# Slot block of a four-stage network: value bias as a matmul, value weights' low parts formed in the second attention, kv affine on two engines, logits ahead of the next hidden layer

## Chip, cores and metric

One core of one Trainium2 chip. The metric is the device time of one execution in microseconds, the median of three runs. Engines are named as in the profile: PE (TensorE), ACT (ScalarE), DVE (VectorE), POOL (GpSimd), SP (SyncE, which here only issues DMAs).

## The reference

Four residual steps on `x` of shape (8, 256, 256) with a context of the same shape:

```python
x = x + tanh(g_xattn[0]) * attention_16_heads(layernorm(x), ctx)
x = x + tanh(g_ffn[0])   * slot_block(layernorm(x))
x = x + tanh(g_xattn[1]) * attention_8_heads(keys and values from ctx and x, queries from x)
x = x + tanh(g_ffn[1])   * int8_like_gated_ffn(layernorm(x))
```

The change touches the second step and the start of the third. The second step, with 64 slots of width 256:

```python
h = gelu(ctx @ w1.T + b1)
route_logits = (h @ w2.T + b2) / (abs(tau) + 0.1)
topk_w = softmax(top 8 of the 64 logits);  alpha = topk_w on those slots, 0 elsewhere
slot_input = einsum('bts,btd->bsd', alpha, x)
gi = slot_input / (alpha.sum(axis=1) + 1e-8)
r, z, n = GRU gates of gi and the slots S
S_new = (1 - z) * n + z * S
slot_values = S_new @ wv.T + bv
out = einsum('bts,bsd->btd', alpha, slot_values) @ wo.T + bo
```

In the third step the keys and values come from `Wkv` (256 x 2048, keys in its first half, values in its second), applied to the context and to the latents, both normed and scaled by `gamma` and `beta` per column; queries come from `Wq`.

## The kernel before

`program` runs four blocks, one behind the other, with a barrier of all engines between them: `attention0`, `slots0`, `attention1`, `ffn1`. Within a block each engine has its own list of instructions, written out by hand, and semaphores between the lists. An engine runs its list strictly in order, so an instruction that waits holds up all behind it.

`slots0` (L951 to L1516) works on four pairs of batches, `p` = 0 to 3, each 512 tokens. The steps and who does them:

- `turn_x(p)` (PE, L1352) transposes the normed tokens, `x_out(p)` (ACT) copies them out, `hidden(p)` (PE, L1360) multiplies by `w1`, `gelu(p)` (ACT, L1056), `logits(p)` (PE, L1368) multiplies by `w2`.
- `logits_out`, `top_eight` (DVE) add `b2` and find the eight largest; `exps(p)` (ACT, L1061); `weights(p)` (DVE, L1190 to L1198) makes `alpha`; `gather(p)` (PE, L1379) forms the slot inputs. gelu and exp use different activation tables, so ACT loads a table between them.
- `gates_of(p)` (PE, L1401 to L1406), `gate_input` (DVE, L1247), `sigmoid` (ACT, L1080), `candidate` (DVE), `tanh` (ACT), `new_slots(p)` (DVE).
- `turn_slots(p)` (PE, L1413), `slots_out(p)` (ACT, L1088), `project_out(p)` (PE, L1419) with `wv` and `wo` folded into one matrix, `slot_values(p)` (DVE, L1268) which adds the folded bias `bvo` and moves the values out of PSUM, `mixture(2p)` and `mixture(2p+1)` (PE, L1427), `residual(b)` (DVE, L1273).
- Meanwhile the block prepares the next one. SP loads `Wq` and `Wkv` into `raw1`; `high(i)` (ACT, L1070, L1072) rounds each of six chunks of 1024 elements per partition to the float32r format, and `low(i)` (DVE, L1280) forms what the rounding left over. Chunks 4 and 5 are the value weights. `c_norm` and `c_apply` (DVE) norm batch 0, `turn_kv(c)` (PE, L1456) transposes it, `kv_affine(c)` (ACT, L1101, L1105) scales it into `kvf` and rounds it, `kv_low(c)` (DVE, L1239) forms its low part.

The order on DVE from the fourth gate input on is, in the code:

```python
            gate_input(3)
            candidate(2)
            new_slots(1)
            low(4)
            candidate(3)
            slot_values(0)
            new_slots(2)
            low(5)
            residual(0)
```

`attention1` begins on PE with keys and queries of two heads (`project_k` L2063, `project_q` L2078), the scores of head 0, and then the first `project_v` (L2089), which reads the value weights. DVE begins with `k_low(0, 0)` (L1813). SP loads a context batch, `bo` and `Wo`, and then the feed-forward weights into the tensors `wih` and `whh`, which `slots0` does not use.

## Time and profile before

| | us |
|---|---|
| median of three runs (lowest, highest) | 895.93 (894.72, 896.11) |
| the profiled execution, its own time | 898.05 |
| span of its trace | 895.9 |
| PE busy in the span | 823.7 (92%) |
| DVE busy | 669.3 (75%) |
| ACT busy | 590.2 (66%) |
| `attention0` | 0 to 213 |
| `slots0` | 213 to 281.5 |
| `attention1` | 281.5 to about 790 |
| `ffn1` | the rest |

A row of the timeline gives the start in us from the span's start, how long the instruction or the merged group lasted, the engine, the line of the kernel, the operation, output and inputs with their shapes, and in brackets how long the engine had been idle and who ended the wait. Successive instructions of an engine overlap a little: the next one starts 0.05 to 0.2 us before the one before it is recorded as done. The granted clock (PEclk) is given as a share of PE's full 2.4 GHz; 0.50 is its lower level, 1.2 GHz.

### The profile page before, as it was taken

To read this page: it belongs to the slowest core of one execution; us is meant where nothing else is said; L and a number is where in the kernel's file an instruction comes from. 1 tells how busy PE (TensorE), PEld (TensorE's weight loads), DVE (VectorE), ACT (ScalarE), POOL (GpSimd) and SP (SyncE) were. 2 spreads that over 40 slices of the span, in tenths; PEclk is the share of its full clock that TensorE was granted. 3 is DMA by queue.
4 is the path that set the end of the run, shared out by engine and by line. 5 is a ranking of instruction groups with operands and counts; after the bars stand their busy time and mean duration, and the time that the engine had idled before them with its cause. 6 is when DMAs were issued, how large, how long until landed. Compare 5 with 4: busy or idle time off the path is not lost. (4 is left out here: it accounts for less than half of the span.)

```text
span 895.9 us, 17186 instructions
## 1 busy us (share of the span) xinstructions
PE 823.7 (92%) x5671; PEld 665.7 (74%) x5671; DVE 669.3 (75%) x1527; ACT 590.2 (66%) x1205; POOL 91.9 (10%) x169
## 2 busy tenths in 40 slices
PE   5899999997886899999999999999899999997757
PEld 5677777665555687888888788888788888885323
DVE  5677888786795778887877686877686877775487
ACT  4366666663733686777787677777577777775663
POOL 4111111010000000100000000000000000000556
PEclk9699999998988999999999999999999999999698
DMA  5832322423103200000000000000000000000002
GB/s 136 143 117 96 98 95 72 139 79 146 9 0 114 61 1 1 13 1 1 13 1 1 16 2 1 13 1 1 16 2 1 1 1 1 1 1 0 1 1 94
DMA packets 37914, 33.41 MB, mean 37 GB/s; under 512 B 10240, under 2 KB 36544, under 8 KB 37568
## 3 DMA queue, kind: packets, MB, share of 16 engines
q1 hardware_dynamic: 37568, 31.76, 12.1%
q0 software_dynamic: 256, 0.52, 0.4%
q8 instruction: 47, 0.77, 0.4%
q14 instruction: 43, 0.35, 0.1%
HBM read 17.59 MB, written 2.10 MB: 22 GB/s over the span
## 5 line engine op out<-in xcount | busy, mean ns | idle before, releaser
L1845 DVE TENSOR_REDUCE c_neg_max<-c_pS 128x1 f32<-128x512 f32 x128 | 88.3, 690 | 70.3 <-PE c_pS L2102 68.9
L1676 ACT ACTIVATE c_probs<-c_pS,c_neg_max 128x512 f32<-128x512 f32 x128 | 88.2, 689 | 62.1 <-DVE c_neg_max L1845 62.1
L547 DVE TENSOR_REDUCE a_neg_max<-a_pS 128x2 f32<-128x512 f32 x128 | 82.4, 686 | 17.1 <-PE a_pS L770 16.6
L1694 ACT ACTIVATE c_probs<-c_probs,c_r_sum 128x512 f32<-128x512 f32 x128 | 92.5, 722 | 3.7 <-DVE c_r_sum L1851 2.9
L400 ACT ACTIVATE a_probsT<-a_pT 128x512 f32<-128x512 f32 x128 | 69.6, 597 | 33.6 <-PE a_pT L786 32.5
L2063 PE MATMUL c_pK<-c_kv,w_hi 128*128 128x512 f32 x256 | 82.9, 406 | 4.6 <-PEq L1515 4.0
L1829 DVE TENSOR_TENSOR c_pT_lo<-c_pT,c_pT_hi 128x512 fp32r<-128x512 f32 x128 | 86.9, 680 | 0.0
L2089 PE MATMUL c_pK<-w_hi,c_kv 128*128 128x512 f32 x248 | 78.9, 399 | 3.2 <-DVE c_k_lo L1813 3.2
L2119 PE MATMUL c_pO<-c_pT_hi,c_v_hi 128*128 128x256 f32 x256 | 77.3, 302 | 3.1 <-DVE c_pT_lo L1829 3.1
L2109 PE MATMUL c_pT<-ident,c_probs 128*128 128x128 f32 x512 | 76.8, 272 | 0.0
L2109 PEld LDWEIGHTS c_pT<-ident,c_probs 128*128 128x128 f32 x512 | 63.6, 140 | 17.5 <-ACT c_probs L1694 0.6
L1684 ACT CAST c_pT_hi<-c_pT 128x512 fp32r<-128x512 f32 x128 | 73.6, 576 | 0.0
L2119 PE MATMUL c_pO<-c_pT_hi,c_v_lo 128*128 128x256 f32 x256 | 72.3, 282 | 0.0
L2119 PE MATMUL c_pO<-c_pT_lo,c_v_hi 128*128 128x256 f32 x256 | 72.1, 282 | 0.0
L2063 PEld LDWEIGHTS c_pK<-c_kv,w_hi 128*128 128x128 f32 x256 | 49.4, 194 | 17.2 <-issue 4.4
L1824 DVE TENSOR_TENSOR c_v_lo<-c_pK,c_v_hi 128x512 fp32r<-128x512 f32 x62 | 42.9, 692 | 21.5 <-ACT c_v_hi L1669 21.5
L1813 DVE SCALAR_TENSOR_TENSOR c_k_lo<-c_pK,c_bk,c_k_hi 128x512 fp32r<-128x512 f32 x64 | 47.3, 739 | 15.3 <-ACT c_k_hi L1658 15.2
L2089 PEld LDWEIGHTS c_pK<-w_hi,c_kv 128*128 128x128 f32 x248 | 45.3, 188 | 18.0 <-DVE c_k_lo L1813 8.3
L1689 ACT ACTIVATE c_oT_hi<-c_pO,c_bv 128x256 fp32r<-128x256 f32 x64 | 30.4, 476 | 41.1 <-PE c_pO L2119 36.6
L2102 PE MATMUL c_pS<-c_k_hi,c_q_hi 128*128 128x512 f32 x128 | 52.8, 412 | 5.0 <-issue 5.0
L2078 PE MATMUL c_pQ<-c_kv,w_hi 128*128 128x256 f32 x256 | 53.8, 303 | 0.0
L2063 PE MATMUL c_pK<-c_kv,w_lo 128*128 128x512 f32 x128 | 51.5, 402 | 0.0
(395 smaller groups left out, 2081.4 us busy)
## 6 DMA issues: line engine op xcount, KB each, us to landing
a_q_stack<-w_hi SPq DMA_DIRECT2D x94, 64.0 KB, 2.6
a_k_stack<-w_hi SPq DMA_DIRECT2D x48, 64.0 KB, 2.6
c_kv<-w_hi SPq DMA_DIRECT2D x42, 64.0 KB, 2.6
s_ctx<-in_ctx_dram SPq DMA_DIRECT2D x8, 256.0 KB, 2.8
x_sb<-in_x_dram SPq DMA_DIRECT2D x8, 256.0 KB, 3.0
b_raw<-in_L_xattn_Wkv_dram SPq DMA_DIRECT2D x1, 2048.0 KB, 12.6
ctx_in<-in_ctx_dram SPq DMA_DIRECT2D x8, 256.0 KB, 2.6
out_dram<-x_sb SPq DMA_DIRECT2D x8, 256.0 KB, 2.2
```

The costliest lines, as they stand in the source:

```text
L400: nc.scalar.activation(probsT[:, r // 2 % 2, 2 * (r % 2) + e, :, :], pT[:, e, :, :], ACT.Exp).then_inc(s["exp"], 1)
L547: nc.vector.tensor_reduce(neg_max[:, r // 2 % 2, :, e, r % 2], pS[:, e, :, :], AX_X, ALU.max, negate=True).then_inc(s["max"], 1)
L1676: nc.scalar.activation(probs[:, u % 2, :], pS[:, u % 2, :], ACT.Exp, bias=neg_max[:, u % 4:u % 4 + 1], accum_out=sums[:, u % 4:u % 4 + 1]) ...
L1684: nc.scalar.copy(pT_hi[:, :, half], pT[:, u % 2, :].rearrange("p (t q) -> p t q", q=P)).then_inc(s["T_hi"], 1)
L1694: nc.scalar.mul(probs[:, u % 2, :], probs[:, u % 2, :], r_sum[:, u % 4:u % 4 + 1]).then_inc(s["probs"], 1)
L1829: nc.vector.tensor_tensor(pT_lo[:, :, half], pT[:, u % 2, :].rearrange("p (t q) -> p t q", q=P), pT_hi[:, :, half].bitcast(F32), ALU.subtr ...
L1845: nc.vector.tensor_reduce(neg_max[:, u % 4:u % 4 + 1], pS[:, u % 2, :], AX_X, ALU.max, negate=True).then_inc(s["max"], 1)
L2063: last = nc.tensor.matmul(pK[:, :], W[x][:, c, INNER + h * DH:INNER + (h + 1) * DH], kv[par][:, y, c, :], start=(c == 0 and i == 0), stop= ...
L2078: last = nc.tensor.matmul(pQ[:, 0:T], W[x][:, c, h * DH:(h + 1) * DH], kv[par][:, y, c, T:KEYS], start=(c == 0 and i == 0), stop=(c == DC ...
L2089: last = nc.tensor.matmul(bank[:, :], kv[par][:, y, c, kt * P:(kt + 1) * P], W[x][:, c, 2 * INNER + half * 512:2 * INNER + (half + 1) * 51 ...
L2109: last = nc.tensor.transpose(pT[:, u % 2, t * P:(t + 1) * P], probs[:, u % 2, t * P:(t + 1) * P], ident[:, :])
L2119: last = nc.tensor.matmul(pO[:, 0:T], (v_hi, v_lo)[x][:, h // 4, t, (h % 4) * DH:(h % 4 + 1) * DH], (pT_hi, pT_lo)[y][:, t, :], start=(t = ...
```

## The change

Five edits:

1. PE issues `logits(p)` ahead of `hidden(p+1)`; the instructions are the same.
2. The folded value bias is put in PSUM by a matmul with the identity, ahead of the projection; ACT (`val_out`) copies the values out, and DVE's `slot_values` is gone.
3. The value half of `Wkv` goes to two further tensors (`raw_v`, the storage of `wih` and `whh`) by two DMAs, `high(4)` and `high(5)` become two casts each, and `low(4)` and `low(5)` leave the block. `attention1` forms these low parts at the head of DVE's list; its first `project_v` of each half waits for them, and so does SP before it loads the feed-forward weights over `raw_v`.
4. `kv_affine` of column 1 is done by DVE; ACT keeps column 0 and both roundings.
5. ACT does `sigmoid(3)` ahead of `tanh(2)`.


```diff
             sp.dma_start(raw1[:, :, 0:INNER], a["L1_xattn_Wq"].rearrange("(c p) n -> p c n", p=P)).then_inc(s["raw"], DMA)
-            sp.dma_start(raw1[:, :, INNER:3 * INNER], a["L1_xattn_Wkv"].rearrange("(c p) n -> p c n", p=P)).then_inc(s["raw"], DMA)
+            sp.dma_start(raw1[:, :, INNER:2 * INNER], a["L1_xattn_Wkv"][:, 0:INNER].rearrange("(c p) n -> p c n", p=P)).then_inc(s["raw"], DMA)
+            for c in range(DC):
+                sp.dma_start(raw_v[c], a["L1_xattn_Wkv"][c * P:(c + 1) * P, INNER:2 * INNER]).then_inc(s["raw_v"], DMA)
...
-                if hi <= INNER:
+                if lo >= 2 * INNER:
+                    if i == 4:
+                        act.wait_ge(s["raw_v"], 2 * DMA)
+                    for c in range(DC):
+                        last = nc.scalar.copy(w1_hi[:, c, lo:hi], raw_v[c][:, lo - 2 * INNER:hi - 2 * INNER])
+                    last.then_inc(s["raw_hi"], 1)
+                elif hi <= INNER:
...
+            def val_out(p):
+                act.wait_ge(s["val"], p + 1)
+                nc.scalar.copy(val[:, p, :], ps[:, p, 0:D]).then_inc(s["val_sb"], 1)
...
             sigmoid(2)
+            sigmoid(3)
             tanh(2)
+            val_out(0)
             slots_out(1)
-            sigmoid(3)
             tanh(3)
+            val_out(1)
             slots_out(2)
+            val_out(2)
             slots_out(3)
-            kv_affine(0)
-            kv_affine(1)
+            kv_affine()
+            kv_high(0)
+            val_out(3)
+            kv_high(1)
...
+            def kv_affine():
+
+                dve.wait_ge(s["kv"], 2)
+                dve.wait_ge(s["snew"], 2)
+                for side in range(2):
+                    last = nc.vector.tensor_scalar(kvf[:, 1, side * T:(side + 1) * T], ps[:, 4, side * T:(side + 1) * T], cols["gamma"][:, side, 1:2],
+                                                   cols["beta"][:, side, 1:2], ALU.mult, ALU.add)
+                last.then_inc(s["kvf1"], 1)
...
             new_slots(1)
-            low(4)
             candidate(3)
-            slot_values(0)
             new_slots(2)
-            low(5)
             residual(0)
...
             def project_out(p):
                 pe.wait_ge(s["snewT_sb"], p + 1)
+                nc.tensor.matmul(ps[:, p, 0:D], ident[:, :], bvo[:, :], start=True, stop=False)
                 for k in range(DC):
-                    last = nc.tensor.matmul(ps[:, p, 0:D], snewT[:, p, k * P:(k + 1) * P], wvo[:, k * D:(k + 1) * D], start=(k == 0), stop=(k == DC - 1))
+                    last = nc.tensor.matmul(ps[:, p, 0:D], snewT[:, p, k * P:(k + 1) * P], wvo[:, k * D:(k + 1) * D], start=False, stop=(k == DC - 1))
...
             turn_x(2)
+            logits(0)
             hidden(1)
-            logits(0)
             turn_x(3)
+            logits(1)
             hidden(2)
-            logits(1)
+            logits(2)
             hidden(3)
-            logits(2)
             logits(3)
...
+            sp.wait_ge(s["w_lo"], 2)
             full = (FT - 1) * P
...
+            for half in range(2):
+                lo, hi = 2 * INNER + half * 512, 2 * INNER + (half + 1) * 512
+                for c in range(DC):
+                    last = nc.vector.tensor_tensor(w_lo[:, c, lo:hi], raw_v[c][:, half * 512:(half + 1) * 512], w_hi[:, c, lo:hi].bitcast(F32), ALU.subtract)
+                last.then_inc(s["w_lo"], 1)
...
                 half, kt = divmod(j, KT)
+                if isinstance(n, int) and n == 0 and kt == 0:
+                    pe.wait_ge(s["w_lo"], half + 1)
```

PE's list in the router, before: transposes of the tokens (from `ident,xn`), the hidden layer (from `b_xT,s_w1T`) and the logits (from `s_w2T,b_hT`).

```order
L1352 MATMUL b_ps<-ident,xn 128x128 x8
L1360 MATMUL b_ps<-b_xT,s_w1T 128x512 x2
L1368 MATMUL b_ps<-s_w2T,b_hT 128x64 x4
L1352 MATMUL b_ps<-ident,xn 128x128 x8
L1360 MATMUL b_ps<-b_xT,s_w1T 128x512 x2
L1368 MATMUL b_ps<-s_w2T,b_hT 128x64 x4
L1360 MATMUL b_ps<-b_xT,s_w1T 128x512 x2
L1368 MATMUL b_ps<-s_w2T,b_hT 128x64 x8
L1434 MATMUL b_ps<-s_whhT,s_ctx 128x512 x2
```

And after:

```order
L1370 MATMUL b_ps<-ident,xn 128x128 x8
L1386 MATMUL b_ps<-s_w2T,b_hT 128x64 x4
L1378 MATMUL b_ps<-b_xT,s_w1T 128x512 x2
L1370 MATMUL b_ps<-ident,xn 128x128 x8
L1386 MATMUL b_ps<-s_w2T,b_hT 128x64 x4
L1378 MATMUL b_ps<-b_xT,s_w1T 128x512 x2
L1386 MATMUL b_ps<-s_w2T,b_hT 128x64 x4
L1378 MATMUL b_ps<-b_xT,s_w1T 128x512 x2
L1386 MATMUL b_ps<-s_w2T,b_hT 128x64 x4
L1453 MATMUL b_ps<-s_whhT,s_ctx 128x512 x2
```

The third group of logits now stands between the last two hidden layers, and each group of logits stands directly behind the transposes or the hidden layer whose output ACT has to turn into its input.

DVE's list in the tail, before, from the last sums of the gate inputs' new slots on: `w1_lo` is a low part of the weights, `b_lm<-b_ps,s_bvo` a value with its bias, `b_ex` new slots.

```order
L1264 TENSOR_TENSOR b_ex<-b_ex_top,b_hT 128x256
L1280 SCALAR_TENSOR_TENSOR w1_lo<-b_raw1,w1_hi 128x2x512
L1252 TENSOR_TENSOR b_hT<-b_xT,s_gh_n 128x256
L1255 TENSOR_TENSOR b_hT<-b_ps,b_hT 128x256
L1268 TENSOR_TENSOR b_lm<-b_ps,s_bvo 128x256
L1260 TENSOR_TENSOR b_ex_top<-s_hs,b_hT 128x256
L1262 TENSOR_TENSOR b_ex_top<-b_ex_top,b_xT 128x256
L1264 TENSOR_TENSOR b_ex<-b_ex_top,b_hT 128x256
L1280 SCALAR_TENSOR_TENSOR w1_lo<-b_raw1,w1_hi 128x2x512
L1273 SCALAR_TENSOR_TENSOR x_sb<-b_ps,gates,x_sb 128x512
```

And after:

```order
L1291 TENSOR_TENSOR b_ex<-b_ex_top,b_hT 128x256
L1279 TENSOR_TENSOR b_hT<-b_xT,s_gh_n 128x256
L1282 TENSOR_TENSOR b_hT<-b_ps,b_hT 128x256
L1287 TENSOR_TENSOR b_ex_top<-s_hs,b_hT 128x256
L1289 TENSOR_TENSOR b_ex_top<-b_ex_top,b_xT 128x256
L1291 TENSOR_TENSOR b_ex<-b_ex_top,b_hT 128x256
L1296 SCALAR_TENSOR_TENSOR x_sb<-b_ps,gates,x_sb 128x512
```

The two low parts and the addition of the bias are gone; the candidate of pair 3, the new slots of pair 2 and the first residual follow one another.

DVE's list at the seam of the two blocks, after: the affine of column 1 (`b_xT` is `kvf`), the low parts of batch 0 (`c_kv0`), and behind the two branches the head of `attention1`.

```order
L1354 TENSOR_SCALAR c_bq<-c_bq 128x8
L1260 TENSOR_SCALAR b_xT<-b_ps,c_gamma,c_beta 128x256 x2
L1266 TENSOR_TENSOR c_kv0<-b_xT,c_kv0 128x512
L1296 SCALAR_TENSOR_TENSOR x_sb<-b_ps,gates,x_sb 128x512 x2
L1266 TENSOR_TENSOR c_kv0<-b_xT,c_kv0 128x512
L957 UNCONDITIONAL_BRANCH
L1784 UNCONDITIONAL_BRANCH
L2015 TENSOR_TENSOR w1_lo<-wih,w1_hi 128x512
L2015 TENSOR_TENSOR w1_lo<-whh,w1_hi 128x512
L2015 TENSOR_TENSOR w1_lo<-wih,w1_hi 128x512
L2015 TENSOR_TENSOR w1_lo<-whh,w1_hi 128x512
L1833 SCALAR_TENSOR_TENSOR c_k_lo<-c_pK,c_bk,c_k_hi 128x512
```

Before, nothing stood between the branches and the first `c_k_lo`, and no `b_xT` was written here.

## Rows read from the trace of the kernel before

**Rows 1.** The page, its first line.

```profile
span 895.9 us, 17186 instructions
```

**Rows 2.** The slot block in the table by stretches (columns: stretch, length, busy time by engine).

```profile
213.00:281.50 68.50, 54.76 (x252) 35.52 (x252) 52.16 (x170) 34.18 (x62) 3.30 (x8) 0.88 0.17 51
```

**Rows 3.** Timeline, PE in the router (start us, us, what, idle before).

```profile
223.30 1.88 PE L1360 MATMUL b_ps<-b_xT,s_w1T 128*128 128x512 f32 x4
225.02 1.00 PE L1368 MATMUL b_ps<-s_w2T,b_hT 128*128 128x64 f32 x8
225.86 1.94 PE L1360 MATMUL b_ps<-b_xT,s_w1T 128*128 128x512 f32 x4
...
233.19 1.10 PE L1379 MATMUL b_ps<-xn,b_alpha 128*64 128x257 f32 x8 [1.74 <-DVE b_alpha L1198]
```

**Rows 4.** Timeline, ACT in the router.

```profile
227.83 0.69 ACT L1056 ACTIVATE b_hT<-b_ps,s_bias 128x512 f32<-128x512 f32 x1 [1.92 <-PE b_ps L1360]
228.54 1.28 ACT L1061 ACT_TABLE_LOAD   x1
229.84 3.18 ACT L1061 ACTIVATE b_ex<-b_lm,b_neg_top,s_tau 128x128 f32<-128x128 f32 x8
```

**Rows 5.** Timeline, DVE in the router.

```profile
231.51 0.43 DVE L1190 TENSOR_TENSOR b_ex_top<-b_ex 128x256 f32<-128x256 f32 x1 [0.74 <-ACT b_ex L1061]
```

**Rows 6.** Stretches of 3 us; PEclk is the third column from the end.

```profile
234.00:237.00 3.00, 2.61 (x15) 1.02 (x11) 2.83 (x20) 3.00 (x6) 0.00 (x0) 0.66 0.02 5
240.00:243.00 3.00, 3.00 (x14) 2.14 (x14) 2.83 (x10) 2.81 (x4) 0.00 (x0) 1.00 0.00 0
258.00:261.00 3.00, 2.34 (x11) 1.53 (x9) 2.90 (x7) 0.42 (x1) 0.00 (x0) 1.00 0.00 0
264.00:267.00 3.00, 3.00 (x12) 1.94 (x9) 2.95 (x5) 0.00 (x0) 0.00 (x0) 0.50 0.00 0
```

**Rows 7.** Groups by line, DVE, 241.5 to 281.5 us.

```profile
L1280 DVE SCALAR_TENSOR_TENSOR w_lo<-b_raw,w_hi 128x1024 fp32r<-128x1024 f32 x6 | 7.3, 1216 | 0.0
...
L1268 DVE TENSOR_TENSOR b_lm<-b_ps,s_bvo 128x256 f32<-128x256 f32 x4 | 1.7, 413 | 0.0
...
L1208 DVE TENSOR_SCALAR b_hT<-b_ps,b_r_wsum 128x256 f32<-128x256 f32 x2 | 1.0, 484 | 0.1
```

**Rows 8.** Timeline, DVE in the tail of the slot block.

```profile
257.79 0.69 DVE L1247 TENSOR_TENSOR b_xT<-b_ps,s_gh_rz 128x512 f32<-128x512 f32 x1 [0.53 <-PE b_ps L1401]
...
261.98 0.42 DVE L1252 TENSOR_TENSOR b_hT<-b_xT,s_gh_n 128x256 f32<-128x256 f32 x1 [0.33 <-ACT b_xT L1080]
...
274.53 1.41 DVE L1273 SCALAR_TENSOR_TENSOR x_sb<-b_ps,gates,x_sb 128x512 f32<-128x512 f32 x2 [0.58 <-PE b_ps L1427]
...
277.74 0.69 DVE L1239 TENSOR_TENSOR c_kv<-b_xT,c_kv 128x512 fp32r<-128x512 f32 x1 [1.40 <-ACT c_kv L1105]
...
279.67 0.68 DVE L1239 TENSOR_TENSOR c_kv<-b_xT,c_kv 128x512 fp32r<-128x512 f32 x1
```

**Rows 9.** Timeline, PE in the tail of the slot block.

```profile
248.37 0.59 PE L1404 MATMUL b_ps<-s_bih,ident 128*128 128x256 f32 x2
248.81 1.03 PE L1406 MATMUL b_ps<-s_wihT,b_turned 128*128 128x256 f32 x4
...
263.25 2.09 PE L1427 MATMUL b_ps<-b_lm,b_turned 64*128 64x256 f32 x8 [2.24 <-DVE b_lm L1268]
...
273.36 1.14 PE L1427 MATMUL b_ps<-b_lm,b_turned 64*128 64x256 f32 x8 [2.49 <-DVE b_lm L1268]
```

**Rows 10.** Timeline, start of the second attention: PE and DVE.

```profile
281.54 1.19 PE L2063 MATMUL c_pK<-c_kv,w_hi 128*128 128x512 f32 x2 [4.03 <-PEq L1515]
...
289.26 0.73 PE L2089 MATMUL c_pK<-w_hi,c_kv 128*128 128x512 f32 x2 [0.16 <-DVE c_k_lo L1813]
...
285.20 0.75 DVE L1813 SCALAR_TENSOR_TENSOR c_k_lo<-c_pK,c_bk,c_k_hi 128x512 fp32r<-128x512 f32 x1 [4.85 <-ACT c_k_hi L1658]
```

More of the change, by code:

```diff
@@ L1092, in values_out, with kv_high @@
                 nc.scalar.copy(wvo, ps[:, 3, :]).then_inc(s["wvo_sb"], 1)
[L1094 to L1099 removed]
+            def val_out(p):
+                act.wait_ge(s["val"], p + 1)
+                nc.scalar.copy(val[:, p, :], ps[:, p, 0:D]).then_inc(s["val_sb"], 1)
+            def kv_affine():
+                act.wait_ge(s["kv"], 1)
+                act.wait_ge(s["cols"], 7 * DMA)
+                act.wait_ge(s["snew"], 2)
                 for side in range(2):
[L1101 to L1102 removed]
+                    last = nc.scalar.activation(kvf[:, 0, side * T:(side + 1) * T], ps[:, 0, side * T:(side + 1) * T], ACT.Identity,
+                                                bias=cols["beta"][:, side, 0:1], scale=cols["gamma"][:, side, 0:1])
                 last.then_inc(s["kvf"], 1)
[L1104 removed]
+            def kv_high(c):
+                act.wait_ge(s[("kvf", "kvf1")[c]], 1)
                 nc.scalar.copy(c_kv[:, 0, c, :], kvf[:, c, :]).then_inc(s["kv_hi"], 1)
@@ L1330, in _ @@
             residual(3)
-            slot_values(2)
             c_apply(2, of_lat, 1, "latn")
@@ L1580, in attention1 @@
         pQ = pb("c_pQ", [P, 512])
-        names = """load next wo wo_hi wo_lo const ctx stats moments var rstd ctxn lat stats_l var_l rstd_l latn kv kvf kv_hi
+        names = """w_lo load next wo wo_hi wo_lo const ctx stats moments var rstd ctxn lat stats_l var_l rstd_l latn kv kvf kv_hi
                    kv_lo k k_hi k_lo q q_hi q_lo v v_hi v_lo S max exp rsum probs T T_hi T_lo O oT_hi oT_lo X ob res stats_o
@@ L2537, in program @@
                 attention0(nc, a, x_sb, ident, gates, {k: v[:] for k, v in gru.items()}, slot, xn, (w1_hi, w1_lo, c_kv))
-                slots0(nc, a, x_sb, ident, gates[:, 2:3], {**slot, "wv": gru["wv"][:]}, xn, w1_hi, w1_lo, ctx_in, clips, c_kv, c_cols)
+                slots0(nc, a, x_sb, ident, gates[:, 2:3], {**slot, "wv": gru["wv"][:]}, xn, w1_hi, w1_lo, ctx_in, clips, c_kv, c_cols, raw_v)
             ident_b = split_w.enter_context(nc.sbuf_tensor("ident_b", [P, P], BF16))
```

26 lines of the change are left out of this document (8 added, 18 removed).

## The prediction

> **What bounds the kernel now.** I read the page first, then the table by stretches, and then the timelines of TensorE (PE), ScalarE (ACT) and VectorE (DVE) over the slot block, asking at each gap who ended it. The profiled execution spans 895.9 us [rows 1], and the change lies almost wholly in the slot block, 213.0 to 281.5 us, where PE is busy 54.8 of 68.5 us and DVE 52.2 [rows 2]: here no engine is full, and what counts is a chain that runs from one to the next. The second attention behind it is left alone but for its first microseconds, so whatever the slot block gains or loses should pass into the time one for one.
>
> The block has two parts for this purpose. In the **router** (to about 233 us) the last link is ACT: it computes the gelu of the four pairs, and only after the fourth can it load the table for exp (1.28 us) and begin the exponentials [rows 4]. DVE waits 0.74 us for the first of them [rows 5], and PE then sits idle for 1.74 us until the first weights `alpha` are there [rows 3]. So gelu(3) starts everything that follows, and gelu(3) waits for hidden(3), which PE begins at 225.86 [rows 3]. In the **tail** (from gate_input(3) at 257.79 [rows 8]) DVE is nearly always busy, and the block ends with DVE's kv_low(1), from 279.67 for 0.68 us. Its only waits there are 0.33, 0.58 and 1.40 us [rows 8]; PE waits 2.24 and 2.49 us for slot values that DVE adds the bias to [rows 9].
>
> **Part 1, logits ahead of the next hidden layer.** Until now PE does hidden(p+1) while ACT does gelu(p), so that logits(p) finds its input ready. Now logits(p) stands first. For p = 0 and 1 another turn_x lies between and little is waited for. For p = 2 nothing does. By PE's rows: turn_x(3) still ends at about 223.4; logits(1) takes 0.85 us (from 225.02 to the next start at 225.86 [rows 3]) and now runs to 224.25; hidden(2) has 1.88 us [rows 3], to 226.15; gelu(2) takes 0.69 us like its sister [rows 4], to 226.9, with PE idle for some 0.9 us; logits(2) 0.85 us, to 227.75; and hidden(3) begins there instead of at 225.86. That is **1.9 us later**, and gelu(3), the table load, the exponentials and `alpha` come as much later. What DVE gains, since logits(0) and logits(1) reach it 1.6 us sooner, is lost, because its next step, weights(0), waits for the exponentials. I see no slack that takes up the 1.9 us: from 231.5 on the four engines pass the work on to each other, and PE's idle 1.74 us is the wait for this very chain. So gather(0), the gates and gate_input(3) move from 257.79 to about 259.7.
>
> **Part 2, low parts of the value weights moved away.** low(4) and low(5) leave DVE's tail: two of the six instructions of 1216 ns [rows 7], 1.14 us each counted to the next start (rows of one engine overlap by some 0.08 us), **2.3 us**. They become four subtractions of 128x512 at the head of the second attention. The nearest row is kv_low, 0.69 us for the same form [rows 8], so 2.5 to 2.8 us in all. There DVE is idle for 4.85 us, of which 3.7 us after the first instruction of PE at 281.54, until the first k_low at 285.20 [rows 10]. I take them at nothing; were this cover gone they would cost up to 2.8 us. The first projection that reads these low parts starts at 289.26 [rows 10], 4 us after they are ready. The new wait stands in SP's queue before the feed-forward weights; they and the load of w_down behind them go out 1 to 2 us later, behind the first three loads of the block, and DVE asks for them only at unit 9 of 16 of the first batch. On ACT high(4) and high(5) become two casts of 128x512 each; both lie between waits of over 2 us. SP issues two DMAs more in the slot block, each 0.4 to 0.6 us of its queue, ahead of loads that are used 20 us later or more: nothing.
>
> **Part 3, bias by a matmul.** The four additions of slot_values leave DVE: 413 ns each [rows 7], 0.34 us counted to the next start, **1.3 us**. PE gets four matmuls with the identity; the same thing for `bih` takes 0.59 us and 0.44 us to the next start [rows 9]. ACT gets four copies of 128x256 out of PSUM. What matters more is that PE no longer has to stand in line behind 1.2 us of low() and the candidate on DVE: its 2.24 and 2.49 us of idle time [rows 9] shrink to the ACT copy of some 0.4 us, though 0.44 us of bias matmul goes in again each time.
>
> **Part 4, affine on two engines, sigmoid(3) ahead.** DVE takes column 1: two tensor_scalar of 128x256 from PSUM, at most 0.48 us each by the form [rows 7], **0.8 us** added. It ends the 1.40 us in which DVE waited for ACT [rows 8], since ACT starts column 0 while DVE is still at the residuals. sigmoid(3) earlier removes the wait of 0.33 us, and the 0.58 us goes with PE's earlier mixtures. That is **2.3 us of waits**; I leave 0.5 us of them in place for the last hand-over, PE's turn_kv to DVE.
>
> **The sum.** Tail: -2.3 (low) -1.3 (bias) -2.3 (waits) +0.8 (affine) +0.5 = -4.6 us. Router: +1.9 us. Together **-2.7 us**. The profiled execution took 898.05 us against a median of 895.93 us of the runs shown, 2.1 us more; so the profiled execution of the new kernel would be about 895.4 and its median **893.2 us**. A measurement of this kernel tells a difference of about 0.2%, 1.8 us, from none.
>
> **What the clock may do to it.** PE's granted clock was 0.66 (a mixture of the levels 2.4 and 1.2 GHz) in 234 to 237, behind the idle 1.74 us, and 0.50, that is 1.2 GHz, in 264 to 267, behind the idle 2.24 us [rows 6]. At 1.2 GHz eight matmuls of a pair of mixtures take 2.09 us, at 2.4 GHz 1.14 us [rows 9]. In the sum I have taken the second spell as gone, because the idle time before it goes, and the first as it was. This is the choice that moves the number most.
>
> **The rivals.** *The slow spell in the tail stays* (0.17). From the first mixture to the end of turn_kv PE has three pairs of mixtures, three projections with bias, two turns and eight transposes: 3.2 + 3.9 + 0.6 + 1.0 = 8.7 us, with the four short waits for ACT about 10.2, against 10.6 us of DVE. A spell of 4 us as before adds about 2 us; turn_kv comes 1.4 us late, and DVE waits at its affine. Then -1.3 us, 894.6.
>
> *The new wait cools PE in the router* (0.10). PE idles some 0.9 us before logits(2) and again before logits(3). If hidden(3) and logits(3) run at 1.2 GHz, 1.72 and 0.85 us become twice that: 2.6 us more on the chain, -0.1 us in all, 895.8. Against it: in 258 to 261 PE was idle for 0.66 of 3 us, and the clock stayed at 1.00 [rows 6]. [...]
>
> *Slower: the clock is low over the router and the gates too* (0.07). Besides those 2.6 us, gates_of(0) would take twice its time: two matmuls of 128x512, 1.72 us as in hidden() (223.30 to 225.02 [rows 3]), 0.44 us for the bias and 0.86 us for two of half the width, 3.0 us, and DVE's gate_input(0) waits for it. -2.7 + 2.6 + 3.0 = +2.9, 898.8. It decides from 4.5 us of extra time on PE's chain on. Against: up to now the clock was back at 1.00 in 240 to 243 [rows 6], before the gates.
>
> *The low parts are not covered in the second attention* (0.03): up to 2.8 us given back, +0.1 at worst, 896.0. For it: DVE would have to start late behind the barrier.
>
> *The reorder is free* (0.08): if hidden(3) were not held up, or gelu(3) not the start of the chain, the tail's gain stands alone, -4.6, 891.3. The rows speak against it.
>
> **How the numbers follow.** The forecast has 0.55, with about 0.8 us to either side for the unknown rests (0 to 1 us of hand-over, 0.7 to 1.0 us of affine). Faster by over 0.2% takes most of it, the free reorder and a little of the slow spell: 0.60. Within: its upper edge, most of the slow spell, the cooled router, the uncovered low parts: 0.32. Slower: 0.08. The range 891.2 to 895.5 reaches from the free reorder to short of the cooled router and leaves out 0.2.
>
> **What would show it.** Right: PE idle of about 0.9 us before logits(2), hidden(3) and gelu(3) 1.9 us later, gather(0) at about 235.1, gate_input(3) at about 259.7; DVE without a gap from there to the affine; the block's last DVE instruction ending at about 277.6; four subtractions on DVE done before 285; granted clock 1.0 from 261 to 270. Wrong: gelu(3) within 0.5 us of 227.83; a wait of over 1 us on DVE for turn_kv; PE below 0.9 of its clock in 243 to 257; the first k_low later than 4 us after the block's start.

## The result, and the profile after

The changed kernel takes **901.84 us** (median of 6 runs, 901.22 to 902.17), the kernel before beside it 896.34 us (6 runs, 894.72 to 897.83): ratio 1.0061, 95% interval 1.0044 to 1.0078. So it is 5.5 us slower, where the forecast was 2.7 us faster. The profiled execution took 901.61 us. Its page, the span and the two queues that carry instructions (packets, MB, share), answers to [rows 1]; the two queue lines of before are 47 packets, 0.77 MB and 43, 0.35.

```profile
span 899.6 us, 17209 instructions
...
q8 instruction: 47, 0.77, 0.4%
...
q14 instruction: 44, 0.35, 0.1%
```

The slot block first. The router, timelines of PE and ACT in after, beside [rows 3, 4]:

```profile
227.56 1.10 PE L1386 MATMUL b_ps<-s_w2T,b_hT 128*128 128x64 f32 x8 [0.78 <-ACT b_hT L1058]
228.50 1.94 PE L1378 MATMUL b_ps<-b_xT,s_w1T 128*128 128x512 f32 x4
231.22 1.10 PE L1386 MATMUL b_ps<-s_w2T,b_hT 128*128 128x64 f32 x8 [0.78 <-ACT b_hT L1058]
...
230.48 0.69 ACT L1058 ACTIVATE b_hT<-b_ps,s_bias 128x512 f32<-128x512 f32 x1 [2.97 <-PE b_ps L1378]
231.18 1.28 ACT L1063 ACT_TABLE_LOAD   x1
232.48 3.18 ACT L1063 ACTIVATE b_ex<-b_lm,b_neg_top,s_tau 128x128 f32<-128x128 f32 x8
```

PE waits 0.78 us before logits(2) and hidden(3) starts at 228.50. gelu(3) starts at 230.48 against 227.83 [rows 4]; the block began 0.42 us later, so the reorder costs 2.2 us here. Then the granted clock, stretches of 3 us as in [rows 6]:

```profile
237.00:240.00 3.00, 2.61 (x12) 1.06 (x11) 2.86 (x20) 3.00 (x7) 0.00 (x0) 0.66 0.03 5
240.00:243.00 3.00, 2.17 (x11) 1.07 (x10) 2.54 (x9) 2.98 (x7) 0.00 (x0) 0.50 0.00 0
243.00:246.00 3.00, 3.00 (x14) 2.23 (x11) 1.81 (x7) 2.54 (x5) 0.00 (x0) 0.70 0.00 0
...
264.00:267.00 3.00, 2.77 (x16) 1.76 (x16) 2.86 (x8) 1.09 (x3) 0.00 (x0) 1.00 0.00 0
```

Behind the wait for `alpha` PE now stays low for about 9 us, where before it was back at 1.00 in 240 to 243; in the tail it never falls. And the tail, DVE, then the PE and ACT rows that one of its waits goes back to, beside [rows 8, 9]:

```profile
261.86 0.69 DVE L1274 TENSOR_TENSOR b_xT<-b_ps,s_gh_rz 128x512 f32<-128x512 f32 x1 [0.53 <-PE b_ps L1419]
...
275.65 0.99 DVE L1260 TENSOR_SCALAR b_xT<-b_ps,c_gamma,c_beta 128x256 f32<-128x256 f32 x2
276.81 0.69 DVE L1266 TENSOR_TENSOR c_kv<-b_xT,c_kv 128x512 fp32r<-128x512 f32 x1 [0.17 <-ACT c_kv L1118]
278.27 1.41 DVE L1296 SCALAR_TENSOR_TENSOR x_sb<-b_ps,gates,x_sb 128x512 f32<-128x512 f32 x2 [0.77 <-PE b_ps L1446]
279.60 0.68 DVE L1266 TENSOR_TENSOR c_kv<-b_xT,c_kv 128x512 fp32r<-128x512 f32 x1
...
277.11 1.14 PE L1446 MATMUL b_ps<-b_lm,b_turned 64*128 64x256 f32 x8 [1.60 <-ACT b_lm L1104]
...
276.17 0.62 ACT L1118 CAST c_kv<-b_xT 128x512 fp32r<-128x512 f32 x1
276.69 0.37 ACT L1104 COPY b_lm<-b_ps 128x256 f32<-128x256 f32 x1
```

From gate_input(3) to DVE's last end it is 261.86 to 280.28, 18.42 us, against 257.79 to 280.35, 22.56: the tail is 4.14 us shorter. What is left in it is a wait of 1.60 us on PE for val_out(3), which ACT has in its queue behind the affine and the first high part; DVE waits 0.77 us for that mixture in turn. The four subtractions at the head of the second attention are free: they run from 281.48 to 284.07, and the first value projection starts at 289.16 against 289.26 [rows 10].

So the block gives back what it wins: +2.2 (router) +1.4 (clock, gather(0) to gate_input(3)) -4.1 (tail) = -0.5 us, and with its start 0.42 us later the second attention begins at 281.48 against 281.54 [rows 10]. **The 5.5 us arise elsewhere**, 215 us further on. A loop of the second attention (batches 1 to 6, two to a turn) jumps back twice. PE's rows at the two jumps, before and then after:

```profile
497.36 0.47 PE L2102 MATMUL c_pS<-c_k_hi,c_q_hi 128*128 128x512 f32 x1 [2.18 <-issue]
631.50 0.76 PE L2102 MATMUL c_pS<-c_k_hi,c_q_hi 128*128 128x512 f32 x1 [2.86 <-issue]
```

```profile
497.38 0.76 PE L2129 MATMUL c_pS<-c_k_hi,c_q_hi 128*128 128x512 f32 x1 [2.31 <-issue]
500.05 0.80 PE L2129 MATMUL c_pS<-c_k_lo,c_q_hi 128*128 128x512 f32 x1 [1.91 <-issue]
...
634.08 0.77 PE L2129 MATMUL c_pS<-c_k_hi,c_q_hi 128*128 128x512 f32 x1 [2.61 <-issue]
636.75 0.79 PE L2129 MATMUL c_pS<-c_k_lo,c_q_hi 128*128 128x512 f32 x1 [1.90 <-issue]
```

"issue" means that PE waited for nothing the trace shows. One such wait per jump has become two, and the view of waits (us in total, times, longest) sums them up, before and after:

```profile
PE c_pS L2102 <- issue: 5.0, 2, 2.9
```

```profile
PE c_pS L2129 <- issue: 8.7, 4, 2.6
```

Aligned instruction by instruction, ACT in after is 0.1 us ahead from 286 to 490, 2.8 us behind from 503 to 620, and 5.6 us behind from 637 on: the two jumps cost 5.7 us more than before. (Behind the last attention 1.8 us of it come back, with the granted clock of 821 to 841 at 0.86 instead of 0.61, so that these two profiled spans differ by 3.7 us and the medians by 5.5.) None of the code there was changed. What did change is the length of PE's list ahead of that loop. From the compiled lists (index of the loop's first instruction; the loop is 1795 instructions long on PE, 347 on DVE):

```
                                    PE     DVE
before                              4558   775
after                               4576   776
```

Four fp32 matmuls with the identity are 4 instructions each, and two waits are added (those of the first `project_v` of each half): 18. The packets of the page don't tell the two kernels apart, 47 and 47: both load instructions at each jump, and only the waits by "issue" show that after waits twice for them.

### The profile page after: what moved, and what is told of

It reads as the page before. It is cut to its first block and busy times, and to the rows that moved or that the text cites. A ratio compares the mean times of both kernels' runs of the same rounds, so it can differ in the third digit from the quotient of the medians.

```text
span 899.6 us, 17209 instructions
## 1 busy us (share of the span) xinstructions
PE 824.3 (92%) x5677; PEld 665.7 (74%) x5679; DVE 669.7 (74%) x1527; ACT 590.4 (66%) x1209; POOL 92.5 (10%) x169
## 5 line engine op out<-in xcount | busy, mean ns | idle before, releaser
L2088 PEld LDWEIGHTS c_pK<-c_kv,w_hi 128*128 128x128 f32 x256 | 49.5, 194 | 16.4 <-issue 3.6
L2129 PE MATMUL c_pS<-c_k_lo,c_q_hi 128*128 128x512 f32 x128 | 51.3, 401 | 3.8 <-issue 3.8
```

What stands on the lines that cost most here:

```text
L2088: last = nc.tensor.matmul(pK[:, :], W[x][:, c, INNER + h * DH:INNER + (h + 1) * DH], kv[par][:, y, c, :], start=(c == 0 and i == 0), stop= ...
L2129: last = nc.tensor.matmul(pS[:, u % 2, :], (q_hi, q_lo)[x][:, slot, qs], (k_hi, k_lo)[y][:, slot, :], start=(i == 0), stop=(i == 2))
```

## The experiments

**Theory F**: each engine fetches its instructions in blocks, and at a jump back it stalls, or not, by where the loop stands in its list; the change only moved it. The rivals were that the new work itself (another wait, a load going out later, the clock) carries into the loop, and for the slot block those of the prediction. In all kernels below the added matmuls write one PSUM column that nobody reads; nothing of the computation is left out in any of them.

### Move PE's list alone

The kernel before, with four matmuls of one column at the end of the slot block's PE list (head of the loop at 4574):

```diff
             mixture(7)
+            pe.wait_ge(s["res"], 4)
+            for _ in range(4):
+                nc.tensor.matmul(ps[:, 5, 0:1], ident[:, :], ident[:, 0:1], start=True, stop=True)
```

> The kernel before, with four one-column matmuls (16 PE instructions in the compiled list) added at the very end of the slot block, where PE idles for over 3 us. Nothing else is changed. Theory F (fetch): what made the changed kernel slower in the second attention is that its 18 extra PE instructions moved the head of PE's loop to just ahead of a border of the instruction stream's fetched pieces, so PE stalls twice on each jump back; then this kernel, moved by 16, shows the second stall of 1.6 to 1.9 us behind the first or second matmul of the iteration on both jumps, and is 3.3 to 4 us slower than before, near 900. Rival W (work): the loss comes from what the change does (waits for low parts, later feed-forward loads, clock); then this kernel takes the time of before, 896.3, within 0.5 us, with one stall per jump.

Measured: **902.66 us** (5 runs, 900.97 to 903.13), ratio 1.0071 [1.0058, 1.0084]. PE at the first jump:

```profile
496.73 0.72 PE L2105 MATMUL c_pS<-c_k_hi,c_q_hi 128*128 128x512 f32 x1 [2.18 <-issue]
...
499.95 0.80 PE L2105 MATMUL c_pS<-c_k_hi,c_q_lo 128*128 128x512 f32 x1 [2.06 <-issue]
```

Sixteen instructions that do nothing make before as slow as after, with a second stall at both jumps (2.06 and 1.49 us). By the medians it is 6.5 us where 3.3 to 4 were expected; aligned with before, this execution loses 5.4 us at the two jumps, after 5.7. Theory F holds, and the change's own work is not needed for the loss. The second stall stands before the third matmul behind the jump here (head at 4574) and before the second in after (head at 4576), which is the same place of the list: index 4583, the weight load of that matmul.

After, with three such matmuls (head at 4588):

> The changed kernel, with three one-column matmuls (12 PE instructions) added at the end of the slot block. Theory F: the loop's head moves past the border, the second stall is gone on both jumps, and the time falls by 3.5 to 4 us from the changed kernel's, to about 898. Rival W: within 0.5 us of the changed kernel, 901.8.

Measured: **892.71 us** (9 runs, 890.49 to 896.03), ratio 0.9960 [0.9947, 0.9973]: 9.1 us less than after, by adding work. I had expected one stall per jump to go; both went, and PE has no issue wait in the loop at all. The page of the profile shows where they went:

```profile
q8 instruction: 29, 0.48, 0.2%
```

29 packets instead of 47. 0.77 MB over 47 packets is 16.4 KB each; 7626 instructions of 64 bytes are 29.8 such blocks, so 29 is the list fetched once, and 18 more are nine blocks for each jump. The Trainium skill (Runtime: NRT & Kernel Launch, section "Instruction fetch mechanics") has the blocks of 256 instructions and says that a taken branch whose target isn't in the current two-block window must fetch it first. The packet size agrees; the two-block window does not: here a loop of seven blocks came back twice without one packet. The same section gives PE's instruction memory as 2048 instructions, which is eight blocks, and that figure fits.

Further places, for the kernel before with 7 and with 24 matmuls (4586, 4654), and the fastest version at that time with 12 (4624):

> The kernel before with seven one-column matmuls (28 PE instructions) and a wait added at the end of the slot block's PE list, so that the head of PE's loop in the second attention stands 28 instructions later, 2 short of where it stands in the stall-free run (after with 3 such matmuls). Theory F (the two jumps back of PE's loop cost by where the head stands, whatever the kernel does): no issue stall of PE at 497 and 632 us, and 2.2 + 2.9 = 5.1 us less than before, about 891 us; since those lie beside half-filled stretches, 3 to 6 us less count. Then the change itself, compared at equal place with the 892.7 us of after with 3 matmuls, is worth between -2 and +2 us. Rival S (the stalls went in that run through the change's own reordering, and not through the place): before keeps one stall per jump, 896 us, or gets two, 902 us.

Measured: **894.11 us** (12 runs, 891.86 to 897.73), ratio 0.9983 [0.9969, 0.9996]. 29 packets, no stall on PE, but only 1.8 us won, not 5: DVE now shows a wait of its own at both jumps,

```profile
497.75 0.69 DVE L1848 TENSOR_REDUCE c_neg_max<-c_pS 128x1 f32<-128x512 f32 x1 [3.58 <-issue]
...
629.73 0.69 DVE L1848 TENSOR_REDUCE c_neg_max<-c_pS 128x1 f32<-128x512 f32 x1 [3.66 <-issue]
```

which in before was covered by the one of PE.

> The kernel before with 24 one-column matmuls (96 PE instructions): the head of the loop 96 instructions later than in before. They take about 24 x 0.06 = 1.5 us on PE at the slot block's end. Theory F with a border (stalls are worst with the head just ahead of a border of 256 instructions, none from just behind it): still no issue stall at the jumps, since the next border is 184 instructions further, and 891 + 0.5 to 1.5 us. Rival (what counts is not a border but the very alignment of the head): one or two stalls per jump, 897 to 904 us.

Measured: **900.07 us** (10 runs, 897.28 to 902.91), ratio 1.0053 [1.0039, 1.0068]. One stall per jump (2.40 and 2.29 us), 48 packets: the "still none" of theory F with a border is wrong. And the matmuls are dearer than I had reckoned:

```profile
278.24 6.14 PE L1515 MATMUL b_ps<-ident 128*128 128x1 f32 x48
```

0.26 us for a matmul (two records each) against the 0.06 us assumed (the four matmuls of the first run had taken 1.05 us already); the second attention starts 4.0 us late, and that is the whole difference from before.

> The fastest version so far with 12 instead of 3 one-column matmuls: 36 PE instructions more ahead of the loop, about 1.1 us more on PE while the vector engine still works, so nearly free. Its head stands between that of the stall-free runs (0 stalls) and that of before plus 24 (one stall per jump). Theory F narrow (stall-free only where the loop's end lies just behind a border, since further in the next block is fetched as well): one stall per jump, 47 or 48 packets on the first instruction queue, 891 to 893 us. Theory F wide (stall-free over a good part of a block): 29 packets, 886.5 to 887.5 us.

Measured: **892.00 us** (6 runs, 891.62 to 892.96), against 886.53 with three: 47 packets, one stall per jump. The stall-free place is narrow: seen at 4586 and 4588, not at 4576 nor at 4624.

The times at which the packets of the first instruction queue start, in the traces, show more. At the first jump they start at 494.46 and 497.72 in before, whose one stall ends at 497.36, and at 494.37 and 497.75 in after, whose stalls end at 497.38 and 500.05. So after waits for the second packet too: with its head seven instructions ahead of 4583 it reaches that border at once. After with three matmuls has no packet between 477 and 759. If a block of 256 begins at 4583, another begins at 6375, and the loop (head + 1795) ends 4 to 22 instructions ahead of that border in the kernels with the head at 4558 to 4576, 6 and 8 behind it at the stall-free 4586 and 4588, 44 and 74 behind it at 4624 and 4654. In the latter two a packet starts 4.4 and 5.3 us before those of the first jump (486.11, 493.20). All this fits an engine that holds eight blocks and loads one ahead: at 4558 to 4576 the head's block is the ninth and gone, and the jump loads nine; just behind the border it is the eighth and still there, unless the next load ahead goes out before the jump. The border and the eight blocks are worked out from these runs after the fact, and no run was made to test them.

### The router's order alone

Before with the new order of logits and hidden, nothing else:

```diff
-            hidden(1)
             logits(0)
+            hidden(1)
...
-            hidden(3)
             logits(2)
+            hidden(3)
```

> The kernel before with the order of the logits of the changed kernel and nothing else; the number of PE instructions is that of before. The chain through gelu(3) says: gelu(3) 2.2 to 2.7 us later, the gates 2.2 us later if PE's clock behaves as before and up to 4 us if the slow spell is as long as in the changed kernel; 898.5 to 900.3. If the reorder were free, 896.3.

Measured: **901.41 us** (6 runs, 897.04 to 902.50), ratio 1.0048 [1.0029, 1.0067]. From the block's start to gelu(3) 16.29 us, as in after (16.27) and against 14.04 in before. From gather(0) to gate_input(3) 26.04 us, against 24.60. The latter is the longer slow-clock spell: over all profiled kernels that distance takes only two values, 24.6 (13 kernels) and 26.0 to 26.2 (5); all three kernels with the new order have the long one, of fifteen with the old order two have it. So the reorder costs 2.2 us, and in these executions 1.4 us more by the clock; that it brings the longer spell about is likely by these counts, but not shown, since the old order can have it as well. The median lies above the expected 898.5 to 900.3: 5.3 us over before, of which these two make 3.6. The profiled execution (902.48 us) began the block 1.7 us later than that of before; the rest of the median's excess is open.

After with the old order put back:

> The changed kernel with the old order of logits and hidden layers. Its tail should be 4 us shorter than before's and its router as before's; the slot block ends 3.5 to 4.5 us earlier than before's, but the loop's head stands where it does in the changed kernel, so by theory F it gives back 3.8 us in the second attention: 896 to 897. By rival W (loss from the waits for low parts) likewise about 896 to 897; by a rival in which the reorder causes the stalls, 892.

Measured: **898.77 us** (6 runs, 897.25 to 900.24), ratio 1.0030 [1.0018, 1.0042]: 3.1 us less than after, but above the 896 to 897 that was expected. The second attention starts at 278.53, 3.0 us before before's (not 3.5 to 4.5: the last mixtures ran at a granted clock of 0.50 here, 2.08 us instead of 1.14), and the kernel is still slower than before, with two stalls at each jump. That is the whole case in one run.

Both together, old order and three matmuls:

> After with the old order of the logits and three one-column matmuls: the tail's gain without the router's loss, at the stall-free place. Measured so far: old order makes after 3.0 us shorter (898.8 against 901.8 us), the place makes it 9.1 us shorter (892.7 against 901.8 us). Theory F (router order and loop place add up): 892.7 - 3.0 = 889.7 us, range 888.5 to 891, second attention starting at 278.5 us, no issue stall at the jumps. Rival (the gain of the slot block is used up on the way, as a wait for something that doesn't start earlier): second attention 3 us earlier but the end within 1 us of 892.7 us.

Measured: **887.76 us** (6 runs, 886.57 to 889.53), ratio 0.9913 [0.9893, 0.9933]. The tail's gain arrives: the second attention starts 3.7 us earlier than in before, and PE has no stall. It is 0.7 us less than the range expected.

### The parts of the tail

Lengths here are from gate_input(3) to the end of DVE's last instruction of the block (before 22.56 us), since they don't depend on the clock in the router.

> Before with one part of the change, the value weights' low parts formed in the second attention (two subtractions of 1.22 us leave the slot block's vector list), and seven one-column matmuls, which put the loop's head where it stands in the stall-free runs. Compared with before plus seven (894.1 us, last vector instruction of the slot block ending at 280.3). By the prediction's term for low (-2.3) and the slow spell in the tail that then goes or stays (-1 to -2 more): last vector end 276.5 to 278, time 890.5 to 892. Rival (the wait for PE takes it over, since residual(0) is then waiting for mixture(0)): end at 279.5 or later, time within 0.8 us of 894.1. By theory F no issue stall at the two jumps and 29 packets on the first instruction queue.

Low parts alone: tail 21.51 us, **-1.05** where the sum had -2.3; 892.18 us (12 runs, 890.08 to 897.72), ratio 0.9957 [0.9941, 0.9973]. PE's wait for DVE's bias addition has its full length and the clock falls behind it as before:

```profile
265.97 1.14 PE L1433 MATMUL b_ps<-b_lm,b_turned 64*128 64x256 f32 x8 [2.24 <-DVE b_lm L1276]
266.00:269.00 3.00, 3.00 (x14) 2.07 (x14) 2.83 (x9) 0.03 (x1) 0.00 (x0) 0.73 0.00 0
```

(The second row is the stretch's clock, 0.73.) Where the other half of the gain went stands in DVE's row for candidate(3):

```profile
264.70 0.43 DVE L1260 TENSOR_TENSOR b_hT<-b_xT,s_gh_n 128x256 f32<-128x256 f32 x1 [1.47 <-ACT b_xT L1088]
```

Its wait for ACT's sigmoid(3) was 0.33 us in before [rows 8]; it has grown by 1.14 us, exactly one low(). So the first of the two low parts stood beside a wait, and its time is won only together with edit 5 of the change, sigmoid(3) ahead, which this run leaves out. In after DVE has no wait there. The end of the last vector instruction, 282.01, is that of the rival (279.5 or later), but this execution also lost 1.1 us in the router and 1.5 us by the long slow-clock spell; the time lies 0.2 us above the other forecast.

> Before with the bias part alone (identity matmul on PE, copy on ACT, four additions of 0.42 us off the vector engine) and three one-column matmuls for the loop's head. By the prediction's term (-1.3): last vector end about 279.0 against 280.3, time 892.8. Rival (bias off the vector engine gains nothing while the low parts still stand there and PE's tail gets four matmuls more): end 279.8 to 280.8, time within 0.5 us of 894.1; rival (val_out(3) ahead of the affine on ACT delays the kv chain): end after 280.8. No issue stall at the jumps, 29 packets.

Bias alone: tail 20.27 us, **-2.29**. DVE's rows add it up: the four additions 1.4, the wait of 0.58 us for the mixtures gone, and the wait for ACT's kv_high 1.08 instead of 1.40 us. So the term of -1.3 was right, and 0.9 us of the waits belong to this part. (This run has val_out(3) ahead of the affine, which after has not; what that order is worth follows below.) PE's waits of 2.24 and 2.49 us are gone (the longest left is 1.58), and the clock stays at 1.00 through the tail. Its time is 887.01 us (6 runs), ratio 0.9899 [0.9884, 0.9914], 7 us under the comparable kernel with low and bias as before, and that is more than the slot block gives. Its DVE list is four instructions shorter (771), DVE's issue wait at the jumps is gone, and the second instruction queue has ten packets fewer. This profiled execution has one stall of PE left:

```profile
q8 instruction: 38, 0.62, 0.3%
q14 instruction: 33, 0.27, 0.1%
```

```profile
627.86 0.47 PE L2106 MATMUL c_pS<-c_k_hi,c_q_hi 128*128 128x512 f32 x1 [3.80 <-issue]
```

38 is 29 and nine, and the times of the same kernel fall in two groups, 886.57 to 887.07 (four) and 891.57 and 892.93 (the profiled one). At this place of the list (4586) the fetch is sometimes needed and sometimes not: this one execution has both, nothing at the first jump and a fetch at the second. There two packets start within 0.4 us (623.08 and 623.50), where the jumps of before and after have one; by the reading above the first is the load ahead, gone out just before the jump. That is argued, not tested.

Next, the old order and three matmuls, with ACT's val_out(3) ahead of its affine, which takes away PE's 1.60 us:

```diff
             slots_out(3)
+            val_out(3)
             kv_affine()
             kv_high(0)
-            val_out(3)
             kv_high(1)
```

> As the run with the old logits and three matmuls, and ACT's val_out(3) ahead of its affine and high part of the contexts' keys. In after PE's mixture(6) waited 1.60 us for it. Theory V (that wait is in the path to the end of the slot block): residual(6) and (7) come 1 to 1.6 us earlier, the kv chain 0.6 us later (one copy ahead of it on ACT), the block ends 0.5 to 1.3 us earlier, 888.4 to 889.2 us if the other run gives 889.7. Rival (the kv chain ends the block as well): block's end unchanged or 0.5 us later, time within 0.5 us of the other run.

Measured: **886.53 us** (5 runs, 886.10 to 887.82), ratio 0.9902 [0.9882, 0.9922]; tail 17.56 us against 18.43 without the move. Theory V holds with 0.9 us by the tails; the times of the two kernels overlap.

The same with both halves of the affine on ACT again, as before the change:

> The fastest version so far (old logits order, three matmuls, val_out(3) early: 886.5 us) with the affine of both channels halves back on ACT, so without the change's split. By the prediction's term the split costs 0.8 us on the vector engine (0.99 us busy) and takes one link of 1.1 us out of ACT's chain: without it the last vector end is 0.5 us later to 0.8 us earlier, 885.7 to 887.0 us. Rival (vector engine would wait 1 us for kv_high(1) before its last subtraction): 887 to 888 us.

Measured: **885.36 us** (4 runs, 883.69 to 885.56), ratio 0.9875 [0.9859, 0.9892]; tail 17.57 us. The split of the affine is worth nothing: DVE saves 0.99 us of work and waits 1.07 us for ACT instead. The 1.2 us less in the time (2.4 by the ratios) come from elsewhere again: three instructions fewer ahead of DVE's loop (773), 33 packets on the second queue, and behind the jump DVE waits for PE only.

```profile
492.99 0.69 DVE L1869 TENSOR_REDUCE c_neg_max<-c_pS 128x1 f32<-128x512 f32 x1 [1.26 <-PE c_pS L2133]
```

### Move DVE's list alone

**Theory G**: DVE's own jump stalls by the same rule. Two memsets of one column at the end of the slot block's DVE list (775 instead of 773):

> The fastest version so far (affine on ACT, 885.4 us) with two memsets of one column added at the end of the slot block's vector list, which then has as many instructions ahead of its loop as before has. Theory G (the vector engine's own jump back stalls by where its list stands, as PE's does): the two c_neg_max behind the jumps wait 3.0 us or more by issue instead of 1.26 us for PE, and the time is 3 to 5 us longer, 888.5 to 890.5 us. Rival (that stall had another cause, as the affine's place): waits 1.26 us for PE as before, 885.0 to 886.0 us.

Measured: **888.81 us** (4 runs, 887.19 to 891.45), ratio 0.9906 [0.9886, 0.9925], 3.4 us more than without. At the second jump

```profile
629.09 0.69 DVE L1872 TENSOR_REDUCE c_neg_max<-c_pS 128x1 f32<-128x512 f32 x1 [3.73 <-issue]
```

and 44 packets on the second queue. (At the first jump this execution had a PE stall of 3.87 us, 38 packets, which covers DVE's.) Theory G holds as to the stall, and the second jump, where PE has none, gives its price: aligned with the kernel without the memsets, 2.1 us. The 3.4 us of the medians can't be put down to DVE alone, since PE's stall by chance is in them; the first jump cost this execution 4.9 us. With 16 and 60 memsets on the split-affine version (792, 836):

> The version with the affine split and val_out(3) early (886.5 us, vector stall of 2.99 us at both jumps) with 16 memsets of one column on the vector engine behind its last work in the slot block (about 16 x 0.06 = 1 us; it would then be idle before the second attention, so it costs 0 to 1 us). Theory G: whether the stall stays depends on the list's place, so either the stall stays (886.5 to 887.5 us) or it goes (882 to 884.5 us). Rival to G: nothing but the 0 to 1 us changes in either this run or the one with 60.

> As the run with 16, with 60 memsets (about 3.6 us, of which 1.2 us lie in the vector engine's idle time at the block's end and the rest delays the four subtractions, needed only at 283 us). Slot block up to 2.5 us longer. Theory G: stall stays, 888 to 890 us, or goes, 884 to 887 us.

Measured: 887.47 us (6 runs, 886.29 to 892.45) and 887.07 us (5 runs, 885.62 to 888.71) against 886.53: the stall stays, at 2.4 to 2.6 us instead of 3.0, with 44 packets each. The memsets were nearly free (0.28 us for 16, 1.09 us for 60), so that the second time lies below both of its forecasts. The two runs show only that 792 and 836 are stalling places too.

Last, that version with the value weights' four subtractions merged into two of 1024 columns (774):

```diff
-            for half in range(2):
-                lo, hi = 2 * INNER + half * 512, 2 * INNER + (half + 1) * 512
-                for c in range(DC):
-                    last = nc.vector.tensor_tensor(w_lo[:, c, lo:hi], raw_v[c][:, half * 512:(half + 1) * 512], w_hi[:, c, lo:hi].bitcast(F32), ALU.subtract)
-                last.then_inc(s["w_lo"], 1)
+            for c in range(DC):
+                last = nc.vector.tensor_tensor(w_lo[:, c, 2 * INNER:3 * INNER], raw_v[c][:, :], w_hi[:, c, 2 * INNER:3 * INNER].bitcast(F32), ALU.subtract)
+            last.then_inc(s["w_lo"], 2)
```

> The version with the split affine and val_out(3) early (886.5 us, c_neg_max waits 2.99 us by issue behind both jumps) with the value weights' low parts formed by two subtractions of 1024 columns instead of four of 512: two vector instructions fewer ahead of the loop, one more than in the stall-free version. Theory G: if the stall goes, c_neg_max waits 1.26 us for PE and the time is 882.5 to 884 us; if it stays, 886 to 887 us with the issue wait of about 3 us. Without theory G: 886 to 887 us and no change in the wait. Rival (the first value projection now waits for the longer subtraction): it would start after 283.5 us, and the time would be up to 0.5 us longer.

Measured: **885.68 us** (4 runs, 884.04 to 886.19), ratio 0.9869 [0.9853, 0.9886]. The wait is gone (1.27 and 1.25 us for PE), with 34 packets. By the medians the gain is 0.9 us of the 3 to 4 expected, and the forecast of 882.5 to 884 us failed. The two kernels were timed beside different medians of before (895.87 and 897.11 us); by the ratios the gain is 2.9 us, though their intervals overlap. The profiled executions agree with that: aligned on ACT, this one is 2.7 us behind at 450, because its slot block began 2.4 us later, and level with the other behind the second jump. So the two jumps are worth 2.7 us.

The main kernels in one table (PE and DVE: index of the loop's head; packets: first and second instruction queue; tail in us; ratio to the runs of before beside them, so that ratios compare better than medians):

| kernel | PE | DVE | packets | tail | median | ratio |
|---|---|---|---|---|---|---|
| before | 4558 | 775 | 47, 43 | 22.56 | 896.34 | 1 |
| after | 4576 | 776 | 47, 44 | 18.42 | 901.84 | 1.0061 |
| before, 4 matmuls | 4574 | 775 | 47, 43 | 22.57 | 902.66 | 1.0071 |
| before, 7 | 4586 | 775 | 29, 43 | 22.56 | 894.11 | 0.9983 |
| after, 3 | 4588 | 776 | 29, 43 | 18.41 | 892.71 | 0.9960 |
| after, old order | 4576 | 776 | 47, 43 | 19.36 | 898.77 | 1.0030 |
| old order, 3 | 4588 | 776 | 29, 44 | 18.43 | 887.76 | 0.9913 |
| ... val_out(3) early | 4588 | 776 | 29, 43 | 17.56 | 886.53 | 0.9902 |
| ... affine on ACT | 4588 | 773 | 29, 33 | 17.57 | 885.36 | 0.9875 |
| ... split, merged low | 4588 | 774 | 29, 34 | 17.57 | 885.68 | 0.9869 |

## Why the prediction was wrong

**The step that failed** is in its first paragraph: "whatever the slot block gains or loses should pass into the time one for one". What the slot block left did pass: ACT was 0.1 us ahead of before up to 490. Then the two jumps back cost 5.7 us more, by 18 instructions added ahead of that loop in PE's list. No term of the sum and no rival had it. The rows were there to see: PE's issue waits of 2.18 and 2.86 us are in the trace of before, at code that I held untouched and did not look at. One rival too few, but also 8 in 100 for "slower" was too little for a sum of -2.7 made of terms of both signs. The sum itself was 2.2 us too good: the slot block gave -0.5 where it had -2.7, and of that 1.4 us are a term put at nothing, the clock behind the router ("the first as it was").

Where each kernel has PE's fetch away (before with 7, after with 3), the change is worth -1.4 us by the medians and -2.1 by the ratios, whose intervals just touch (0.9969 to 0.9996 and 0.9947 to 0.9973). Even that is not the slot block's: both profiles have it at 66.5 us. DVE's two stalls are 3.0 us long in the one and 3.6 in the other, 1.2 us together.

*Router, +1.9.* The mechanism was right, the place too; it measured 2.2 us, since hidden(2) started 0.2 us later than worked out and logits(2) takes 0.94 us to the next start, not 0.85. What the sum had at nothing, the clock behind it, cost 1.4 us more. The rival "the new wait cools PE in the router" did not come true as stated: behind waits of 0.78 us the clock stayed at 1.00; the longer low spell came behind the old idle 1.74 us.

*Tail, -4.6.* It measured -4.1, and the slow spell there went, as forecast. The terms hold in the rows of after: two low() of 1.14 us and four additions are gone, the affine costs 0.99 us of DVE for the 0.8 of the sum, and 0.94 us of waits are left for its 0.5. What was wrong is that they stand by themselves. The low parts alone gave -1.05 for -2.3, because the wait for sigmoid(3) took up one of them; the bias alone gave -2.3 for -1.3, because 0.9 us of the waits are its own; and the split of the affine gave 0.0, since the wait that it ends (1.07 us) is as long as its work, where the sum had a gain of 1.4 less 0.8. Bias on PE was the part that ended PE's waits of over 2 us and with them the half clock. What sigmoid(3) ahead is worth by itself was not run.

*Low parts in the second attention, 0.* Right: over at 284.07, cover until 289.16. *The last hand-over, 0.5.* 0.17 and 0.77 us of waits were left; the larger was an order on ACT that I had not read against PE's queue.

*Gates at 259.7.* 261.86, by the router's 0.3, the block's 0.4 and the clock's 1.4 us. *Last DVE end at 277.6.* 280.28, by the same and the tail's 0.4.

## What to carry to other kernels

When a change adds or removes even a few instructions ahead of a hardware loop, compare the waits by "issue" at the loop's jumps in both profiles, and the packets of the instruction queues (which here tell a jump that loads from one that doesn't, not one stall from two), before anything is credited to the change; a version that only adds idle instructions ahead of the loop separates the two in one run. Each engine jumps back for itself and the longest stall hides the others, so removing one pays only down to the next. A part of a change that is run alone can lose its gain to a wait that another part removes: compare the waits, not only the length. And a gain in one stage that starts the next one earlier (3.0 us here) can still end in a slower kernel: follow the difference instruction by instruction to the end.

## What the runs showed that I had not expected

- A jump back of PE's loop (1795 instructions) cost 0, one stall of 2.1 to 3.9 us, or two of 1.5 to 3.0 us, by its place in the list: one at 4558, 4624 and 4654, two at 4574 and 4576, at 4586 and 4588 mostly none and in two profiled executions one. Each jump that stalls fetches nine packets of 16.4 KB. DVE's loop (347 instructions): none at 771, 773 and 774, 2.9 to 3.7 us from 775 to 777, 2.4 to 2.6 us at 792 and 836, with ten packets of some 8 KB more on the second queue. That the stalls are the fetch is shown by the packets that come and go with them, and for PE's second stall by the packet's time. The rule of places given above for PE is untested, and for DVE none was found. ACT shows issue waits of 1.7 to 3.0 us at these jumps in all eighteen kernels; its list was not moved by itself.
- The longer slow-clock spell is all or nothing: the distance from gather(0) to gate_input(3) was 24.6 or 26.1 us and never between; the fifteen kernels with the old order of the logits have nearly the same program there, and thirteen of them have the short one.
- The fastest versions found, 885.4 and 885.7 us, contain the change without its new order of the logits, 1.8% under after. The former is also without its split affine; both rest on the place of the list, and a later edit ahead of the loop can lose up to 9 us of it.
